# A hybrid transformer block on one core: routing a batch inside the next batch's attention instead of in a stage of its own

## What is computed

```python
x = x + _L0_attn_a_ref(_layernorm(x), ...)      # 16 heads of 64, 64 features
x = x + _L0_ffn_ref(_layernorm(x), ...)         # 160 experts, 8 of them a token
x = x + _L0_attn_b_ref(_layernorm(x), ...)      # causal softmax attention
x = x + _L0_ffn_ref(_layernorm(x), ...)
```

```python
probs = sigmoid(x @ router_w.T + expert_bias)
top_w, top_idx = top_k(probs, 8)                # top_w is scaled to the sum 2.5
routed = sum over the 8 of top_w * (silu(x @ w_gate[e].T) @ w_down[e].T)
out = routed + silu(x @ w_gate_shared.T) @ w_down_shared.T
```

## Time and profile before

| what | us |
|---|---|
| median of three runs | 2910.31 |
| the profiled execution | 2888.6 |
| its span | 2887.3 |
| `key_maximum` | 0 to 111 |
| attention of batches 0, 1, 2, 3 from | 112, 326, 546, 761 |
| `route` of batches 0, 1, 2, 3 from | 278, 491, 713, 929 |
| first experts | 987 to 1350 |
| `layer_b` | 1350 to 2270 |
| second route and experts | 2277 to 2887 |

### The profile page before, as it was taken

One profiled execution on the slowest core, in us unless ns is written; L12 is line 12 of the kernel. 1 busy time (PEld: TensorE's weight loads), 2 busy tenths in 40 slices (PEclk: granted clock), 3 DMA queues, 4 the chain that ended last, 5 costly groups with the idle time before them and its releaser, 6 DMA issues. The chain is left out here.

```text
span 2887.3 us, 45561 instructions
## 1 busy us (share of the span) xinstructions
PE 1992.7 (69%) x15787; PEld 1142.0 (40%) x15787; DVE 1664.6 (58%) x4731; ACT 1049.6 (36%) x2016; POOL 1306.3 (45%) x1340
## 2 busy tenths in 40 slices
PE   5896696696696577664878788987988657766000
PEld 3455355255355355452333333433333335554000
DVE  5466566657567533355786787688785443245222
ACT  0253253253253245442355544434444234443000
POOL 0042265365465343554345540551454634356775
PEclk9898798698798599887687786787787679788555
DMA  9200000000003466664222121211200556565221
GB/s 378 86 1 4 15 15 23 22 18 20 28 16 158 154 209 202 193 189 144 53 70 65 50 64 25 60 54 43 58 32 23 207 191 209 189 194 179 72 60 46
DMA packets 132475, 275.69 MB, mean 95 GB/s; under 512 B 29411, under 2 KB 44387, under 8 KB 127891
## 3 DMA queue, kind: packets, MB, share of 16 engines
q1 hardware_dynamic: 99478, 205.60, 21.6%
q0 software_dynamic: 32768, 67.17, 7.7%
HBM read 146.34 MB, written 125.93 MB: 94 GB/s over the span
## 5 line engine op out<-in xcount | busy, mean ns | idle before, releaser
L859 POOL DMA_INDIRECT slots_in<-g_xs,g_place x512 | 503.8, 984 | 462.8 <-issue 119.3
L2199 ACT ACTIVATE b_pT<-b_psE 128x512 f32<-128x512 f32 (+3 forms) x768 | 326.6, 490 | 452.9 <-PE b_psE L2096 399.4
L1896 DVE TENSOR_REDUCE b_peak<-b_psM 128x1 f32<-128x512 f32 (+3 forms) x768 | 393.3, 550 | 145.0 <-PE b_psM L2084 88.2
L884 POOL DMA_INDIRECT r_xs<-slots_out,g_place x336 | 334.9, 997 | 226.8 <-ACT b_pT L2199 96.6
L2079 PE MATMUL b_psM<-b_kS,b_qS 72*128 72x512 bf16 (+3 forms) x640 | 242.4, 391 | 58.5 <-DVE b_peak L1896 33.0
L2096 PE MATMUL b_psE<-b_qS,b_kS 75*128 75x512 bf16 (+3 forms) x768 | 245.2, 397 | 44.5 <-ACT b_pT L2199 39.4
L884 POOL DMA_INDIRECT g_xs<-slots_out,g_place x176 | 173.6, 987 | 138.2 <-issue 46.4
L2108 PE MATMUL b_psV<-b_pT,b_vb 128*32 128x512 f32 (+3 forms) x1536 | 207.1, 622 | 23.9 <-POOL b_pT L2263 22.0
L1446 DVE COPY m_staged_w<-wgd 128x192 f32 x512 | 98.3, 264 | 203.6 <-PE m_psY L1388 113.0
L1446 DVE COPY n_staged_w<-wgd 128x192 f32 x512 | 97.1, 261 | 204.4 <-PE n_psY L1388 144.0
L2263 POOL TENSOR_SCALAR_AFFINE_SELECT b_pT<-b_pT 128x512 f32<-128x512 f32 x128 | 82.3, 643 | 206.9 <-ACT b_pT L2199 205.3
(11 more groups left out here) (518 smaller groups left out, 4221.4 us busy)
## 6 DMA issues: line engine op xcount, KB each, us to landing
wgd<-in_w_gdT SPq DMA_DIRECT2D x8, 3840.0 KB, 23.0
slots_in<-g_xs SPq DMA_DIRECT2D x26, 1024.0 KB
m_rows<-slots_in SPq DMA_DIRECT2D x104, 256.0 KB
slots_out<-m_y SPq DMA_DIRECT2D x104, 256.0 KB
n_rows<-slots_in SPq DMA_DIRECT2D x104, 256.0 KB
slots_out<-n_y SPq DMA_DIRECT2D x104, 256.0 KB
b_qS<-q_parts SPq DMA_DIRECT2D x48, 192.0 KB
b_kS<-k_parts SPq DMA_DIRECT2D x48, 192.0 KB
```

The costliest lines, as they stand in the source:

```text
L859: self.nc.gpsimd.indirect_dma_start(self.G.slots_in[self.h], bass.IndirectOffsetOnAxis(self.G.place[:, TPH * self.h + t, k:k + 1], 0), sel ...
L884: self.nc.gpsimd.indirect_dma_start(self.rows(i)[:, k, :], None, self.G.slots_out[t // TPH], bass.IndirectOffsetOnAxis(self.G.place[:, t, ...
L1896: nc.vector.reduce_max(to, taking()[:, 0:size], AX.X).then_inc(m_taken, 1)
L2199: nc.scalar.activation(pT[:, e % KEPT, h, q0:HALF], psE[:, j % BANKS, q0:HALF], ACT.Exp, scale=SCALE).then_inc(e_taken, 1)
```

## The change

There are two edits.

The first takes the `route` stages of batches 0, 1 and 2 out of the program. The pieces of routing that `layer_b` had (`route_batch` with its `norm`, `take_turned`, `turn_rows`) become functions of the module (`route_on_vector`, `norm_pieces`, `turned_pieces`, `turn_on_tensor`, `route_on_tensor`), with their buffers and semaphores in an object `R` (`routing`). `attn_a` of b = 1, 2, 3 calls them for batch p = b-1. On VectorE a key tile has 8 slots, and a slot takes one piece: two behind `kf`, two behind the sum of squares (which is now a function apart from the argument), four behind the argument. A piece that needs a result of TensorE takes it from bank 3 of `psB`; TensorE fills this one bank 13 times (14 where p is 1), each time in the place of its own stream that the slot's number gives (`FILLED_AT`), and waits before it for VectorE to have taken what was there. `add_kv` is cut in two halves so that a place lies between them. ScalarE does the sigmoid of the logits and that of the shared expert's hidden values, in place of one Silu; the load of Sigmoid's table and the return to Exp's come with it. VectorE leaves six slots without a piece behind the request for the sigmoids. The routing's buffers lie partly in `prod`, `qs` and `qsT`. Four small loads on SyncE's queue and five small constants on GpSimd come to each of the three stages. `fold_output`, which writes to bank 3, waits for the last take. GpSimd sends the batch's scatters from query tile 2 on, three ahead of each `weigh` (18 in all, the first behind a wait for `placed`), then 15 in the feed-forward stage and the rest in the key part of the attention after that, 4 a tile. The fourth `route` stage stays. Of batch 2, 53 of 64 are out when the first experts begin, where all had been.

The second edit is in `maximum` of `layer_b`: the diagonal tile's columns are made by the same matmul as those left of them, and only the mask keeps a matmul of its own. Where before there were 640 matmuls of L2079 and 512 of L2082, there are 768 in all; the columns are as many.

```diff
-SEND_A_KEY_TILE, SEND_IN_FFN, SEND_IN_ROUTE = 4, 4, 5
+SEND_A_KEY_TILE, SEND_A_QUERY_TILE, SEND_IN_FFN, SEND_IN_ROUTE = 4, 3, 5, 5
+FIRST_SEND = 2
...
+def norm_pieces(nc, dve, R, x, to, ready, free=None):
+
+    stats, moments, var, half_var, rstd = R.stats, R.moments, R.var, R.half_var, R.rstd
+    nc.vector.drain()
...
+    yield from turned_pieces(nc, dve, R, take, R.rT_ready)
+    yield
+    for t0, t1 in RANKED:
+        nc.vector.tensor_tensor(logits[:, t0:t1, :], take()[:, 0:(t1 - t0) * EXPERTS].rearrange("p (t e) -> p t e", e=EXPERTS),
+                                bias[:].unsqueeze(1).to_broadcast([P, t1 - t0, EXPERTS]), ALU.add).then_inc(m_taken, 1)
+        yield
...
+    nc.vector.drain()
+    dve.sem_inc(R.sig_ready, 1)
+    sigmoid_here()
+    for _ in range(6):
+        yield
+    dve.wait_ge(R.sig_done, n + 1)
...
+def attn_a(nc, stage, G, A, N, b, W, S, scatters):
...
+    SLOTS = 8
+    FILLED_AT = (0, 1, 2, 3, 4, 4, 5, 6)
+    TAKES = 13 + p % BPH if b else 0
+    taken, sigmoid_at = set(), []
...
+            R = routing(nc, m, prod[0:INTER, 0, :], prod[0:INTER, 1, :], qs[:, 0, :], N.stats, N.mv, N.var, N.half, N.rstd,
+                        probs=queries[:, 0:TPB * EXPERTS].rearrange("p (t e) -> p t e", e=EXPERTS),
+                        picked=qs[:, 1, 0:TPB * EXPERTS // 2].bitcast(BF16).rearrange("p (t e) -> p t e", e=EXPERTS),
+                        before=queries[:, TPB * EXPERTS:TPB * EXPERTS + (TPB + 1) * EXPERTS // 2].bitcast(BF16).rearrange("p (t e) -> p t e", e=EXPERTS),
+                        ends=qs[:, 1, TPB * EXPERTS // 2:TPB * EXPERTS // 2 + 2 * EXPERTS].rearrange("p (a e) -> p a e", e=EXPERTS))
+            made = m.sem("made")
...
+            def key_square_sums(t):
+                dve.wait_ge(k_squared, t + 1)
+                nc.vector.reduce_sum(shift[:], sq[:, t % 2, :].rearrange(heads, k=DH), AX.X).then_inc(k_diag, 1)
+                nc.vector.drain()
+
+            def key_argument(t):
+                dve.wait_ge(kd_done, t + 1)
+                if t >= 2:
+                    dve.wait_ge(k_exp, t - 1)
+                nc.vector.tensor_tensor(arg[:, t % 2, :].rearrange(heads, k=MF), dash, bc(shift[:], MF), ALU.subtract).then_inc(k_arg, 1)
...
+            def take():
+
+                assert now[0] not in taken
+                taken.add(now[0])
+                dve.wait_ge(R.m_done, len(taken))
+                return psB[:, 3, :]
+
...
+            now, pieces = [0], routed() if b else iter(())
+
+            def side(t, slots):
+                for i in slots:
+                    now[0] = SLOTS * t + i
+                    next(pieces, None)
+
+            for t in range(TPB):
+                if t:
+                    key_features(t - 1)
+                side(t, (0, 1))
+                key_square_sums(t)
+                side(t, (2, 3))
+                key_argument(t)
+                side(t, range(4, SLOTS))
+            key_features(TPB - 1)
+            while len(taken) < TAKES:
+                now[0] += 1
+                next(pieces)
...
-                if send:
-                    send(SEND_A_KEY_TILE)
+                if b >= 2:
+                    scatters[(b - 2) // BPH].of_batch(b - 2)(SEND_A_KEY_TILE)
...
+                if b:
+                    if t == FIRST_SEND:
+                        pool.wait_ge(R.placed, 1)
+                    if t >= FIRST_SEND:
+                        scatters[p // BPH].of_batch(p)(SEND_A_QUERY_TILE)
...
+                if b:
+                    pe.wait_ge(R.m_taken, TAKES)
...
+            filled = [0]
+
+            def use():
+                if filled[0]:
+                    pe.wait_ge(R.m_taken, filled[0])
+                filled[0] += 1
+                return psB[:, 3, :]
+
+            pieces = route_on_tensor(nc, pe, G, R, p, 0, use) if b else None
+
+            def fill(t, place):
+
+                for i, at in enumerate(FILLED_AT):
+                    if at == place and SLOTS * t + i in taken:
+                        next(pieces)
+
             for t in range(TPB):
+                fill(t, 0)
                 if t:
                     values(t, 0)
+                fill(t, 1)
                 key(t)
+                fill(t, 2)
                 if t:
                     values(t, 1)
+                fill(t, 3)
                 key_dash(t)
+                fill(t, 4)
                 if t:
-                    add_kv(t - 1)
+                    add_kv(t - 1, range(HA // 2))
+                    fill(t, 5)
+                    add_kv(t - 1, range(HA // 2, HA))
                 else:
                     values(0, 0)
+                    fill(t, 5)
                     values(0, 1)
+                fill(t, 6)
...
+            def sigmoids(slots):
+
+                if sigmoid_at and sigmoid_at[0] in slots:
+                    act.wait_ge(R.sig_ready, 1)
+                    nc.scalar.activation(R.probs[:], R.logits[:], ACT.Sigmoid)
+                    nc.scalar.activation(R.hsig[:], R.hs[:], ACT.Sigmoid).then_inc(R.sig_done, 1)
...
-                edge = n - P if diagonal else n
-                if edge:
-                    last = nc.tensor.matmul(ps[:, 0:edge], qS[0:STACK, g, h, qt * P:(qt + 1) * P],
-                                            kS[0:STACK, g, h, kh * HALF:kh * HALF + edge], start=True, stop=True)
+                last = nc.tensor.matmul(ps[:, 0:n], qS[0:STACK, g, h, qt * P:(qt + 1) * P],
+                                        kS[0:STACK, g, h, kh * HALF:kh * HALF + n], start=True, stop=not diagonal, skip_group_check=diagonal)
                 if diagonal:
-                    nc.tensor.matmul(ps[:, edge:n], qS[0:STACK, g, h, qt * P:(qt + 1) * P],
-                                     kS[0:STACK, g, h, kh * HALF + edge:kh * HALF + n], start=True, stop=False)
-                    last = nc.tensor.matmul(ps[:, edge:n], ident_bf[:], mask_q[:], start=False, stop=True)
+                    last = nc.tensor.matmul(ps[:, n - P:n], ident_bf[:], mask_q[:], start=False, stop=True, skip_group_check=True)
...
-                    for b in range(BATCH - 1):
+                    for b in range(BATCH):
+                        attn_a(nc, f"a{b}_", G, weights, N, b, W, S["m"], scatters)
+                        assert b < 2 or scatters[(b - 2) // BPH].sent >= TPB * TOPK * ((b - 2) % BPH + 1)
                         send = scatters[(b - 1) // BPH] if b else None
-                        attn_a(nc, f"a{b}_", G, weights, N, b, send)
-                        ffn_a(nc, f"f{b}_", G, F, N, b, send)
-                        route(nc, f"m{b}_", G, W, *part(b), send)
-                        assert b == 0 or send.sent == TPB * TOPK * ((b - 1) % BPH + 1)
-                    send = scatters[1]
-                    attn_a(nc, "a3_", G, weights, N, BATCH - 1, send)
+                        if b < BATCH - 1:
+                            ffn_a(nc, f"f{b}_", G, F, N, b, send)
...
```

795 lines of the change are left out of this document (413 added, 382 removed).

## The result

The changed kernel takes 2907.71 us (median of 20 runs, 2892.65 to 2914.82), the kernel before 2916.39 us (20 runs). The ratio is 0.9962, with a 95% interval of 0.9947 to 0.9976: 7 to 15 us faster, where 55 were forecast. The profiled executions are 2888.6 us before and 2892.65 us now.

What follows compares the result with a forecast made beforehand. It took the `route` stages to be bound by an uncovered VectorE chain. Terms: -149.1 removed, +59 key parts, +36 queries, +1 experts, -2 `layer_b`, so -55 us: 2855 us from 2910.31, own range 2822 to 2887, 8 in 10 within 2812 to 2892.

Steps and rivals of the forecast that it cites:

- What was removed: `route` stages of batches 0, 1 and 2: they go, and the next attention starts about 1 us behind; -149.1 us.
- The key part: Attention's key tiles with routing beside them: 17 us more, 25 for batch 1; +59 us in all, bounds +30 to +80.
- the price of the hand-offs through the one bank: Key part: 13 or 14 fills and takes a batch through one PSUM bank, given 2 us a batch.
- The upper bound of +80: Key parts: cover fails for half of the routing and a third of the hand-offs wait, +80 us.
- The query part: Attention's query tiles: GpSimd's scatters make it the bound at 8.76 us a tile; +36 us, bounds 27 to 42.
- experts +1: First experts: they begin with 11 scatters more behind them; +1 us, 0 to +4.
- `layer_b` -2: 384 matmuls go while their columns stay, worth a little hand-over; -2 us, bounds 0 to -19.
- The 11 us estimated from the back-to-back gap: `layer_b`: by the skill page's 81 ns spacing, 384 fewer matmuls would be worth near -11 us; not the term used.
- Dear hand-offs: Rival: TensorE and VectorE wait in turn at the one bank; key parts +80, queries +42; 2887 us, chance 0.10.
- The fallen clock: Rival: TensorE's waits inside key tiles drop its clock to half speed; 3038 us, chance 0.05.
- Better cover: Rival: only TensorE's +30 shows in the key parts and +27 in the queries; 2818 us, chance 0.09.
- no gain: Rival: routing pieces run behind the keys, the chain as long as before; within 0.2% of 2910 us, chance 0.02.

Runs made afterwards that it cites:

- e9: Changed kernel with VectorE's MAX8 and index search done twice in the attention; ratio 1.0038 to the kernel before, key parts 97.9, 103.6 and 97.9 us.
- e11: Changed kernel with the shared expert's additions earlier and some of TensorE's bank 3 fills later; ratio 0.9943 to the kernel before, key parts 82.2, 93.7, 86.7 us.
- e14: Changed kernel with VectorE's seven readings of bank 3 in key tiles 1 and 2 done twice; ratio 1.0012 to the kernel before.
- e3: Kernel before with only the second edit, the merged matmul in `maximum` of `layer_b`; ratio 1.0002 to the kernel before.

## Why the prediction was wrong

**What was removed** was right: the three stages are gone, and the next attention's keys start 1.0 to 1.1 us behind the feed-forward's last operation.

**The key part** is the term that failed: +59 forecast, +92.6 measured, 34 of the 42 us that are missing in the first layer. The mechanism, VectorE becoming the bound once the search begins, was right (e9). The step that failed is the price of the hand-offs through the one bank, 2 us a batch, and with it the rule that in tiles 0 to 2 the larger of the engines' times counts.

The halves at tile 3's sum of squares show where it went. In tiles 3 to 7 I let VectorE's load of 47.9 us replace five tiles of 7.57, which adds 10.0 us to batch 1; it was 17.8 (33.6 to 51.4), with VectorE busy 78% of the time and not over 80. TensorE stands at a fill in its own order, the keys of the next tile stand behind it, and VectorE waits for them afterwards. With the fills and takes moved it is 10.5 us (e11), so VectorE's load was sized rightly and the hand-offs cost 7.3 us there, 4.5 and 5.1 in batches 2 and 3, matmuls at half clock behind the waits included. In tiles 0 to 2 I added 5 us of TensorE's work and 2.5 at the sigmoids; 9.7 to 11.4 came (27.9 to 39.3 in batch 1). There the turning, the logits and the shared expert go through one bank, filled and taken seven times in a row, and VectorE's takes count nearly in full although TensorE is the busier engine (e14).

Two smaller errors are in the sums. The 62.94 us of the key part reach 1.4 us into the queries; from the 61.5 us up to them the same sum is +18.6 a batch, not +17. And the range's lower end, 2822, isn't what the terms' lower bounds give (30 + 27 + 0 - 19 us back, 2799). The upper bound of +80 assumed that a third of the hand-offs wait; it was too low as well.

**The query part**: +36 forecast, +44 measured, 2 us over the upper bound. The mechanism holds, shown by the runs with one scatter less at a time: 8.76 us a tile by my rows, 9.0 to 9.2 measured. I had taken the second fold at its mean of 1.245 us, while beside VectorE's `qs` it takes 1.60, as the one of 1.59 in the earlier trace rows did. And I let 2 of the 14 us be covered; all of them showed.

**The rest**: experts +1 agrees with 268.4 against 268.5 us on the quick chip. `layer_b` -2 agrees with 0 within 4 us by the times of whole runs (e3); in the profiles of the changed kernel the stage takes 951.5 to 961.7 us, so a single pair of profiles couldn't have shown it. The 11 us estimated from the back-to-back gap didn't come.

**The rivals.** Dear hand-offs is what happened, given 0.10, at 2887 us; by the first layer alone it is 2898, and 2907.71 was measured. The start of the sum was low too: over 20 runs the kernel before takes 2916.39 us, not 2910.31. The rival's price was my error: it took the upper ends of terms whose ends were too near. The fallen clock came in part only: 0.89, 0.87 and 0.87 in the key parts against 0.97, below the 0.9 that the prediction named as a sign against itself. Matmuls ran at half speed for a few us behind waits of 2 to 8 us and at full speed otherwise. By the groups that took longer in batch 1's (3.28, 2.04, 2.02 and 3.53 us instead of 1.88, 1.16, 1.11 and 1.88) that is some 5 of the 29 us, an upper estimate, since no run tested how much of it lies on the path. Better cover and no gain fell.

## What to carry to other kernels

A chain that moves beside other work through one buffer can cost more than the larger of the two engines' times: 39.3 us went by here with TensorE busy 33.3 and VectorE 21.2. Count each fill and take as a round trip of both, and ask what each engine has in its own order behind the wait. A helper engine has a pace too: add its instructions per tile and compare with the cadence before putting more there; the first scatter a tile was free, and each further one cost nearly its full time. And a long wait in the trace is not its price: either edit against the wait of 7.56 us gave 2 to 3 us, since another wait took its place, and only both together gave 8.5.

## What the runs showed of the hardware

VectorE's two-input `qs` ran 4.49 us instead of 1.23 beside GpSimd's product and fold, and ended 1.1 us after the first fold did; a scatter beside it took 1.69 us instead of 0.97. The Trainium skill, "SBUF — State Buffer", section "SBUF: two separate sides", has the two engines share a port pair that one instruction holds to its end, for VectorE operations with two SBUF inputs against GpSimd operations that read SBUF. The trace agrees: `qs` ends about one operation's length after GpSimd's.

The same instructions settled into a tile of 7.1 us (two profiles on quick chips) or of 7.5 us (one profile on a slower chip), 3 us a key part, at a granted clock of 0.96 to 0.97 in both. Chips differed by 7% in the time of the whole kernel, and most of that lies in the stages of experts, where the first took 264 to 271 or 339 to 355 us.
